# An attention block on one core: in every fourth step the weighting moves behind the scores, and all of v between the first and the second products

## The chip, the core and the metric

One core of a Trainium2 chip runs the whole program. Its engines work side by side, each on its own list of instructions, and wait for each other by semaphores: PE (TensorE, matrix products), DVE (VectorE), ACT (ScalarE), POOL (GpSimd), and SP (SyncE), which here only issues DMAs. The metric is the device time of one execution in microseconds (us). The kernel before took 781.42 us, the median of three runs (779.24 to 783.10).

## The reference

A modulated layer norm goes into attention with 16 heads over quantised weights, and a second one into a dense layer with routed low-rank experts. Shapes: x is (4, 512, 256), a head is 128 wide, features are 16 x 128.

```python
mod = (silu(c) @ wmod).reshape(4, 6, 1, 256)      # sa, ca, ga, sb, cb, gb
ga = sign(ga) * max(abs(ga), 0.25)                # gb likewise
h = layernorm(x) * (1 + ca) + sa
q, k, v = (h @ (codes_m * repeat(scales_m, 32, axis=0)) + b_m for m in "qkv")
scores = einsum("bqhd,bkhd->bhqk", q, k) / sqrt(128)
attn = softmax(scores)
out = einsum("bhqk,bkhd->bqhd", attn, v).reshape(4, 512, 2048)
x = x + ga * (out @ (wo_codes * repeat(wo_scales, 32, axis=0)) + bo)
h = layernorm(x) * (1 + cb) + sb
# 8 experts, the two best per token, weights normalised and times 16
y = h @ W.T + sum_e(weight_e(h) * (h @ A_e.T) @ B_e.T)
x = x + gb * y
```

Results are float32. The kernel keeps that precision on PE by splitting each operand into a high part (rounded) and a low part (what is left): each product is three matmuls, high x high, high x low and low x high.

## The kernel before, in words

**Steps.** Heads are taken in 8 pairs. For each pair there are 8 steps, one for each of 4 batches and 2 heads, so 64 steps in all. Step s of pair p has number n = 8p + s, and t = s % 4 is its place in a cycle of four. "First step" means t = 0 and "fourth step" t = 3. The first pair and the last are written out, the others run in a loop (pair 1 is written out on POOL, ACT and DVE too).

**What a step holds.** PE makes the scores of step n (4 tiles of 128 rows, 12 matmuls of 512 columns, function scores), the weighting of step n-2 with v (weighted, 12 matmuls of 512), v for the next step (next_v, 12 matmuls of 256) and the output projection of step n-2 (out_projection, 12 of 256). Between these lie the q and k projections of coming steps. They are made for two batches together by seven block products instead of eight, each with 3 matmuls of 512 columns for q and 3 for k (product). A fourth step has products 1 and 2 (function first_outputs), a first step products 6, 7 and 4, second and third steps one each.

**The way of a softmax tile.** DVE takes the row maximum (maximum, L1353), ACT the exponentials (exps, L887), DVE transposes blocks of 32 (turn, L1368), SP moves the blocks to their partitions with 16 DMAs a step (L449, pB to pT), ACT makes the high part (prob_high, L818), POOL the low part (prob_low, L581, tile pT_parts), and only then can PE weight (weighted waits for p_lo_ok of each of its 4 key tiles kt). The last turn of a step waits for o_mm, the end of PE's weighting in the same step.

**A fourth step before** (first_outputs, L1886): scores; product 1 for q and k, into the banks score0 and score1, each behind a wait for the exponentials of that tile (exp_ok); the weighting; product 2 for q and k, behind ACT's copies of product 1 (kept_ok); v; the output projection. The next step's scores wait for q_ok and k_ok. These come from ACT's q_high and k_high (L796, L800, after product 2) and DVE's q_low and k_low (L1250, L1255). ACT's order after the exponentials is: two copies of product 1, o_high, q_high, k_high, v_out, four high parts (first_cycle_step, prob_and_v). DVE's is: the turns, o_low, q_low, k_low, v_low, y_add (which adds the output projection to y_acc), then the next maxima.

**The last pair** has the second half's preparations on POOL and DVE. gate(b) multiplies y_acc by ga, add_gated_bo(b) adds ga * bo to x_nat, attended(b) (L1342) adds the two, statistics(b) takes row statistics and variances, inverse_std (POOL) makes 1/std, and times_gb(b) scales the dense and expert weights by gb. In step 4 of this pair DVE does attended(0) and statistics(0) between o_low and q_low. In step 7 POOL does add_gated_bo(3) and times_gb(1) to (3). After step 7 come the last two weightings (weighted_end) with low parts from DVE (hT_lo, L1348 and L1556), and then the dense layer, router and experts.

## Time and profile before

| what | value |
|---|---|
| median of 3 runs | 781.42 us (779.24 to 783.10) |
| profiled execution: its own time, its span | 782.79 us, 780.8 us |
| PE busy | 757.5 us (97%) |
| DVE, POOL, ACT busy | 660.9 (85%), 623.9 (80%), 562.5 us (72%) |
| mean granted TensorE clock | 0.995 |

The span goes from the first to the last instruction; 2.0 us of the execution's own time lie outside it. Matmuls overlap, so a busy share of PE says that it was fed and not that it ran at its peak. What shows a loss on PE is the distance between the starts of two matmuls: 0.23 us for 512 columns and 0.12 us for 256 where nothing is waited for. The granted clock is the share of full speed that PE was given.

### The profile page before, as it was taken

How to read it: one execution, taken by the hardware profiler on the slowest of the kernel's cores; microseconds unless marked ns; L12 is line 12 of the kernel's file. 1: busy time of each engine (PE TensorE's matmuls, PEld its weight loads, DVE VectorE, ACT ScalarE, POOL GpSimd, SP SyncE). 2: the span in 40 equal slices, each digit the busy share in tenths (PEclk: the TensorE clock that was granted, in tenths of full speed). 3: DMA queues.
4: the chain of work that ended last, by engine and by line, in shares of the span. 5: the costliest groups of instructions: out<-in, count | busy, mean ns of one | idle time of the engine just before them, and what ended most of it. 6: DMA issues, size and time to landing. Idle time of an engine off the chain costs nothing.

```text
span 780.8 us, 15093 instructions
## 1 busy us (share of the span) xinstructions
PE 757.5 (97%) x4128; PEld 650.9 (83%) x4128; DVE 660.9 (85%) x1268; ACT 562.5 (72%) x1226; POOL 623.9 (80%) x654
## 2 busy tenths in 40 slices
PE   8999999999999999999999999999999999989898
PEld 7888878787888888888888888888888888878697
DVE  7899989888797988888797988888797988898976
ACT  4787777777777777777777777777777777767641
POOL 4488789898688987898688987898688987988932
PEclk9999999999999999999999999999999999999999
DMA  8354434543455344543445344543445345662202
GB/s 259 91 148 125 97 81 135 136 108 94 108 142 146 91 103 128 144 125 91 112 135 151 91 104 127 141 128 91 112 135 152 91 102 133 162 176 70 49 1 108
DMA packets 71725, 92.20 MB, mean 118 GB/s; under 512 B 19477, under 2 KB 36598, under 8 KB 71670
## 3 DMA queue, kind: packets, MB, share of 16 engines
q1 hardware_dynamic: 52368, 73.21, 36.4%
q10 hardware_dynamic: 19302, 18.42, 8.0%
q8 instruction: 15, 0.25, 0.1%
q14 instruction: 40, 0.33, 0.1%
HBM read 23.39 MB, written 2.11 MB: 33 GB/s over the span
## 4 chain that ended last, share of the span: by engine, by line
PE 56%; SPq 12%; DVE 11%; issue 7%; POOL 7%; ACT 3%; DMA 2%; ACTq 1%; DVEq 0%; POOLq 0%
SPq L449 12%; PE score L1587 8%; PE score L1589 7%; PE score L1588 7%; PE o L1587 5%; PE o L1589 5%; PE o L1588 5%; POOL pT_parts L581 3%; DVE pB L1368 3%; DMA pT<-pB 2%; DVE y_acc L1322 2%; PE qv L1587 2%; PE qv L1589 2%; PE qv L1588 2%; DVE neg_max L1353 2%
## 5 line engine op out<-in xcount | busy, mean ns | idle before, releaser
L581 POOL TENSOR_TENSOR pT_parts<-pT,pT_hi 128x512 fp32r<-128x512 f32 x248 | 315.4, 1307 | 94.0 <-ACT pT_hi L818 93.9
L887 ACT ACTIVATE prob<-score,neg_max 128x512 f32<-128x512 f32 x256 | 173.3, 687 | 47.2 <-DVE neg_max L1353 45.4
L1368 DVE STREAM_TRANSPOSE pB<-prob 128x512 f32<-128x512 f32 x252 | 162.4, 686 | 48.7 <-PE o L1589 47.6
L1353 DVE TENSOR_REDUCE neg_max<-score 128x1 f32<-128x512 f32 x256 | 159.6, 680 | 1.0 <-PE score L1589 0.8
L818 ACT ACTIVATE pT_hi<-pT 128x512 fp32r<-128x512 f32 x248 | 135.6, 621 | 9.9 <-DMA pT<-pB 9.7
L1587 PE MATMUL score<-k_hi,q_hi 128*128 128x512 f32 x256 | 101.8, 398 | 3.7 <-DVE k_lo L1255 2.7
L1588 PE MATMUL score<-k_lo,q_hi 128*128 128x512 f32 x256 | 100.8, 394 | 0.0
L1589 PE MATMUL score<-k_hi,q_lo 128*128 128x512 f32 x256 | 100.3, 392 | 0.0
L1587 PE MATMUL o<-pT_hi,v_hi 128*128 128x512 f32 x248 | 96.8, 390 | 0.0
L1589 PE MATMUL o<-pT_hi,v_lo 128*128 128x512 f32 x248 | 96.6, 389 | 0.0
L1588 PE MATMUL o<-pT_parts,v_hi 128*128 128x512 f32 x248 | 96.6, 389 | 0.0
L808 ACT ACTIVATE o_hi<-o 128x512 fp32r<-128x512 f32 x62 | 37.2, 600 | 61.2 <-PE o L1589 60.9
L1587 PE MATMUL score<-wv_hi,hT_hi 128*128 128x256 f32 x228 | 64.6, 284 | 0.8 <-POOL wv_lo L656 0.8
L1589 PE MATMUL score<-wv_hi,hT_lo 128*128 128x256 f32 x228 | 64.5, 283 | 0.0
L1588 PE MATMUL score<-wv_lo,hT_hi 128*128 128x256 f32 x228 | 64.5, 283 | 0.0
L1286 DVE TENSOR_TENSOR v_lo<-score,v_hi 128x512 fp32r<-128x512 f32 x57 | 39.3, 689 | 25.2 <-ACT v_hi L804 25.2
L1587 PEld LDWEIGHTS score<-k_hi,q_hi 128*128 128x128 f32 x256 | 48.5, 189 | 13.9 <-issue 4.7
L804 ACT ACTIVATE v_hi<-score 128x512 fp32r<-128x512 f32 x57 | 34.1, 599 | 35.4 <-PE score L1589 35.1
L1589 PEld LDWEIGHTS score<-k_hi,q_lo 128*128 128x128 f32 x256 | 48.4, 189 | 10.7
L1587 PEld LDWEIGHTS o<-pT_hi,v_hi 128*128 128x128 f32 x248 | 46.5, 188 | 10.5 <-POOL pT_parts L581 0.7
L1588 PEld LDWEIGHTS score<-k_lo,q_hi 128*128 128x128 f32 x256 | 48.6, 190 | 7.5
L1589 PEld LDWEIGHTS o<-pT_hi,v_lo 128*128 128x128 f32 x248 | 46.6, 188 | 9.7
(458 smaller groups left out, 2016.1 us busy)
## 6 DMA issues: line engine op xcount, KB each, us to landing
pT<-pB SPq DMA_DIRECT2D x1008, 64.0 KB, 2.0
x_nat<-in_L_attn_x_dram ACTq DMA_DIRECT2D x4, 512.0 KB, 5.0
out_dram<-x_nat SPq DMA_DIRECT2D x8, 256.0 KB, 2.3
stage<-in_L_attn_wv_codes_dram ACTq DMA_DIRECT2D x7, 256.0 KB
stage<-in_L_attn_wv_scales_dram ACTq DMA_DIRECT2D x14, 128.0 KB
stage<-in_L_attn_wq_codes_dram ACTq DMA_DIRECT2D x7, 256.0 KB
stage<-in_L_attn_wq_scales_dram ACTq DMA_DIRECT2D x14, 128.0 KB
stage<-in_L_attn_wk_codes_dram ACTq DMA_DIRECT2D x7, 256.0 KB
```

The costliest lines, as they stand in the source:

```text
L449: sp.dma_start(flat(pT32[32 * g:32 * (g + 1), par, a]), flat(pB[32 * a:32 * (a + 1), par, g])).then_inc(p_land[par], 16)
L581: pool.tensor_tensor(turned(par, kt, pT_lo), turned(par, kt), split(pT_hi, kt).bitcast(f32), ALU.subtract).then_inc(p_lo_ok, 1)
L804: act.activation(v_hi[:, par, 2 * half:2 * half + 2, :], v_view(bank), ACT.Copy).then_inc(v_hi_ok, 1)
L808: act.activation(by_tile(o_hi[:, :]), in_token_order(bank[:, :]), ACT.Copy).then_inc(o_hi_ok, 1)
L818: act.activation(split(to, kt), turned(par, kt), ACT.Copy).then_inc(p_hi_ok, 1)
L887: act.activation(prob[:, i], score_ps[i][:, :], ACT.Exp, bias=neg_max[:, i:i + 1], accum_out=row_sum[:, s % 2, i:i + 1]).then_inc(exp_ok, 1)
L1286: dve.tensor_tensor(v_lo[:, par, tiles], v_view(bank), v_hi[:, par, tiles].bitcast(f32), ALU.subtract).then_inc(v_lo_ok, 1)
L1353: dve.tensor_reduce(neg_max[:, i:i + 1], score_ps[i][:, :], AX.X, ALU.max, negate=True).then_inc(max_ok, 1)
L1368: dve.transpose(pB[:, s % 2, :, :, i].rearrange("p g k q -> p k g q"), prob[:, i].rearrange("p (k g q) -> p k g q", k=QT, g=G)).then_inc(p ...
L1587: pe.matmul(dst, a_hi, b_hi, start=first, stop=False, skip_group_check=joins)
L1588: pe.matmul(dst, a_hi, b_lo, start=False, stop=False, skip_group_check=joins)
L1589: return pe.matmul(dst, a_lo, b_hi, start=False, stop=last, skip_group_check=joins)
```

## The change

1. Fourth steps, PE (first_outputs): the weighting comes straight behind the scores, then product 1, then both tiles of v, then product 2, then the output projection.
2. Fourth steps, ACT: o_high before the copies of product 1, v_out before q_high and k_high; the high part of the v weights (v_weights_high, steps 7) behind the exponentials instead of before them. DVE: v_low before q_low and k_low.
3. POOL, steps 1 and 2 of each pair from pair 1 on: the low parts of the mixed q and k (mixed_low, L570) before the parts of the output weights instead of behind them.
4. First pair: in step 6 POOL's first q part waits for q_mm alone, and ACT makes the high part of input mix 4 behind the four high parts of the weights; in step 7 DVE's input_mix(0, 3) goes from before the last turn to behind o_low.
5. Last pair: POOL's add_gated_bo(2) in step 4 waits for attended(0) (x1_ok); DVE's variances(0) go behind k_low; in step 7 POOL does times_gb(1) and then waits for DVE's four low parts (p_lo_dve); add_gated_bo(3), times_gb(2) and times_gb(3) go further back.

The same computation is done; no instruction is added or taken away on PE, DVE, ACT or POOL but for waits.

```diff
@@ POOL, first pair
                     elif s == 6:
                         input_mix_lo(0, 2)
+                        pool.wait_ge(q_mm, SPP)
+                        parts_1("q", 1)
                         pool.wait_ge(k_mm, SPP)
-                        parts_1("q", 1)
                         parts_1("k", 1)
@@ POOL, pair
                     elif s < 3:
+                        for m in "qk":
+                            mixed_low(m, u3 if s == 1 else u2, mixed)
                         pool.wait_ge(y_mm, DC * (n - 2))
                         parts("o", p, 2 - s)
...
                         elif s == 4:
                             gate(0)
+                            pool.wait_ge(x1_ok, 1)
                             add_gated_bo(2)
...
                         else:
-                            add_gated_bo(3)
                             times_gb(1)
-                            times_gb(2)
-                            times_gb(3)
+                            pool.wait_ge(p_lo_dve, QT)
...
-                    if s % 4 in (1, 2):
+                    if s in (5, 6):
                         for m in "qk":
-                            mixed_low(m, u3 if s % 4 == 1 else u2, mixed)
+                            mixed_low(m, u3 if s == 5 else u2, mixed)
@@ POOL, after the last pair
             inverse_std(B + 1)
+            add_gated_bo(3)
             gate(2)
...
             pool.tensor_tensor(x_nat[:, rows], y_acc[:, rows], x_nat[:, rows], ALU.add).then_inc(x1_ok, 1)
+            times_gb(2)
             inverse_std(B + 2)
+            times_gb(3)
             inverse_std(B + 3)
@@ ACT, first_cycle_step
                 made = cycle(p, s // 4) + 1
+                o_high(n - 1)
                 first_copied("q", made + 1)
                 first_copied("k", made + 1)
-                o_high(n - 1)
+                v_out(n + 2, batch_of((s + 1) % SPP) % 2, (s + 1) % 2)
                 q_high(SPP + 2 * made + 1, 0, first_ps["q"])
                 k_high(SPP + 2 * made + 1, 0, first_ps["k"])
                 if isinstance(p, int) and p == 0:
                     input_mix_hi(0, 3)
-                prob_and_v(p, s)
+                prob_high((s - 1) % 2, landed(p, s - 1))
@@ DVE, pair
                     if last and s == 4:
                         attended(0)
-                        statistics(0)
+                        for i in range(QT):
+                            row_statistics(0, i)
...
                         k_low(SPP + 2 * now, head_at(p, s + 1))
+                        if last and s == 4:
+                            variances(0)
                     elif t == 3:
+                        v_low(n + 2, batch_of(nxt) % 2, nxt % 2)
                         q_low(SPP + 2 * now + 1, head_at(p, s + 1), first_ps["q"])
                         k_low(SPP + 2 * now + 1, head_at(p, s + 1), first_ps["k"])
-                    v_low(n + 2, batch_of(nxt) % 2, nxt % 2)
+                    if t < 3:
+                        v_low(n + 2, batch_of(nxt) % 2, nxt % 2)
@@ PE, first_outputs
+                weighted_ready(p, s)
+                weighted(n - 2, s % 2, batch_of(s - 2) % 2, j)
                 for i, m in enumerate("qk"):
                     if s == SPP - 1:
                         pe.wait_ge(w_ok[m], parts_of(m, p + 1) + 1)
                     pe.wait_ge(exp_ok, QT * n + i + 1)
                     product(first_ps[m], m, 1, b, True).then_inc(product_mm[m], 1)
-                weighted_ready(p, s)
-                weighted(n - 2, s % 2, batch_of(s - 2) % 2, j)
+                next_v(p, s)
                 for m, done in (("q", q_mm), ("k", k_mm)):
                     pe.wait_ge(kept_ok[m], kept("copy", made))
                     product(first_ps[m], m, 2, b, False).then_inc(done, 1)
-                next_v(p, s)
                 out_projection(p, s)
```

PE at the end of the scores in the fourth step of the loop's first half (score<-k is a score matmul, score<-hT_hi,wq_hi a matmul of product 1, o<-pT_hi one of the weighting). Before:

```order
L1589 MATMUL score<-k_hi,q_lo 128x512
L1892 ISA
L1893 REGISTER_ALU
L1587 MATMUL score<-hT_hi,wq_hi 128x512
L1588 MATMUL score<-hT_lo,wq_hi 128x512
L1589 MATMUL score<-hT_hi,wq_lo 128x512
```

And of the changed kernel, at the same place and then from the end of v:

```order
L1597 MATMUL score<-k_hi,q_hi 128x512
L1598 MATMUL score<-k_lo,q_hi 128x512
L1599 MATMUL score<-k_hi,q_lo 128x512
L1597 MATMUL o<-pT_hi,v_hi 128x512
L1598 MATMUL o<-pT_parts,v_hi 128x512
L1599 MATMUL o<-pT_hi,v_lo 128x512
```

```order
L1599 MATMUL score<-wv_hi,hT_lo 128x256
L1909 ISA
L1597 MATMUL score<-hT_hi,wq_hi 128x512
L1598 MATMUL score<-hT_lo,wq_hi 128x512
L1599 MATMUL score<-hT_hi,wq_lo 128x512
L1597 MATMUL score<-hT_hi,wk_hi 128x512
L1598 MATMUL score<-hT_lo,wk_hi 128x512
L1599 MATMUL score<-hT_hi,wk_lo 128x512
L1867 MATMUL y<-wo_hi,o_hi 128x256
L1868 MATMUL y<-wo_lo,o_hi 128x256
```

The weighting, which stood six matmuls behind the last score matmul, is now its neighbour, and product 2 has only the output projection between it and the next scores.

ACT in the fourth step of the last pair (o_hi is o_high, qv and ky from score the copies of product 1). Before:

```order
L887 ACTIVATE prob,row_sum<-score,neg_max 128x512 x4
L823 ACTIVATE qv<-score 128x512
L823 ACTIVATE ky<-score 128x512
L808 ACTIVATE o_hi<-o 128x512
L796 ACTIVATE q_hi<-score,bias_now 128x512
L800 ACTIVATE k_hi<-score,bias_now 128x512
L804 ACTIVATE v_hi<-score 128x512
L818 ACTIVATE pT_hi<-pT 128x512 x4
```

And of the changed kernel:

```order
L892 ACTIVATE prob,row_sum<-score,neg_max 128x512 x4
L813 ACTIVATE o_hi<-o 128x512
L828 ACTIVATE qv<-score 128x512
L828 ACTIVATE ky<-score 128x512
L809 ACTIVATE v_hi<-score 128x512
L801 ACTIVATE q_hi<-score,bias_now 128x512
L805 ACTIVATE k_hi<-score,bias_now 128x512
L823 ACTIVATE pT_hi<-pT 128x512 x4
```

o_hi moved before the two copies, and v_hi before q_hi and k_hi.

DVE in step 4 of the last pair (x_nat<-y_acc,x_nat is attended(0), BN_STATS to var_eps the statistics). Before:

```order
L1291 TENSOR_TENSOR o_lo<-o,o_hi 128x512
L1342 TENSOR_TENSOR x_nat<-y_acc,x_nat 128x1024
L1148 BN_STATS stats<-x_nat 128x6 x4
L1154 BN_AGGR mv<-stats 128x2 x4
L1159 TENSOR_SCALAR var_eps<-mv 128x4
L1250 SCALAR_TENSOR_TENSOR q_lo<-qv,vecT,q_hi 128x512
L1255 SCALAR_TENSOR_TENSOR k_lo<-ky,vecT,k_hi 128x512
L1286 TENSOR_TENSOR v_lo<-score,v_hi 128x512
```

And of the changed kernel:

```order
L1297 TENSOR_TENSOR o_lo<-o,o_hi 128x512
L1348 TENSOR_TENSOR x_nat<-y_acc,x_nat 128x1024
L1154 BN_STATS stats<-x_nat 128x6 x4
L1256 SCALAR_TENSOR_TENSOR q_lo<-qv,vecT,q_hi 128x512
L1261 SCALAR_TENSOR_TENSOR k_lo<-ky,vecT,k_hi 128x512
L1160 BN_AGGR mv<-stats 128x2 x4
L1165 TENSOR_SCALAR var_eps<-mv 128x4
L1292 TENSOR_TENSOR v_lo<-score,v_hi 128x512
```

The variances moved from before q_lo to behind k_lo; attended(0) and the row statistics stay where they were.

## Rows read from the trace of the kernel before

**Rows 1.** The page, busy time, share of the span and instructions of each engine:

```profile
PE 757.5 (97%) x4128; PEld 650.9 (83%) x4128; DVE 660.9 (85%) x1268; ACT 562.5 (72%) x1226; POOL 623.9 (80%) x654
```

**Rows 2.** Who waited for whom on PE: us in total, times, longest:

```profile
PE score L1587 <- ACT prob L887: 10.3, 14, 1.5
...
PE score L1587 <- DVE k_lo L1255: 2.7, 1, 2.7
```

**Rows 3.** PE in order of time, one fourth step: start us, us, engine, line, operation:

```profile
408.07 0.40 PE L1587 MATMUL score<-k_hi,q_hi 128*128 128x512 f32 x1
...
410.60 0.39 PE L1589 MATMUL score<-k_hi,q_lo 128*128 128x512 f32 x1
...
411.64 0.50 PE L1587 MATMUL score<-hT_hi,wq_hi 128*128 128x512 f32 x1 [0.66 <-ACT prob L887]
...
411.98 0.39 PE L1588 MATMUL score<-hT_lo,wq_hi 128*128 128x512 f32 x1
...
417.00 0.39 PE L1589 MATMUL score<-hT_hi,wk_lo 128*128 128x512 f32 x1
...
420.10 0.40 PE L1587 MATMUL score<-k_hi,q_hi 128*128 128x512 f32 x1
```

**Rows 4.** In order of time, the weights' low parts against the scores, two fourth steps:

```profile
408.83 5.06 POOL L581 TENSOR_TENSOR pT_parts<-pT,pT_hi 128x512 fp32r<-128x512 f32 x4 [1.52 <-ACT pT_hi L818]
...
451.95 0.40 PE L1587 MATMUL score<-k_hi,q_hi 128*128 128x512 f32 x1
...
452.63 5.05 POOL L581 TENSOR_TENSOR pT_parts<-pT,pT_hi 128x512 fp32r<-128x512 f32 x4 [1.45 <-ACT pT_hi L818]
```

**Rows 5.** The chain that ended last, in order of time: start us, us, what:

```profile
439.76 0.72 DVE pB L1368
...
449.91 1.98 DMA pT<-pB
```

**Rows 6.** In order of time, the end of k in a first step:

```profile
430.16 0.39 PE L1589 MATMUL ky<-gb_row_parts,wk_lo 128*128 128x512 f32 x1
...
431.32 0.75 DVE L1255 SCALAR_TENSOR_TENSOR k_lo<-ky,vecT,k_hi 128x512 fp32r<-128x512 f32 x1
```

**Rows 7.** In order of time, v in the fourth step of the first pair:

```profile
104.48 1.28 POOL L656 TENSOR_TENSOR wv_lo<-stage,wv_hi 128x512 fp32r<-128x512 f32 x1
...
105.81 0.39 PE L1587 MATMUL score<-wv_hi,hT_hi 128*128 128x256 f32 x1 [0.77 <-POOL wv_lo L656]
```

**Rows 8.** In order of time, the last pair's fifth step into its sixth:

```profile
692.31 2.40 POOL L607 TENSOR_TENSOR x_nat<-x_nat,ga_bo 128x1024 f32<-128x1024 f32 x1
...
692.44 3.35 DVE L1342 TENSOR_TENSOR x_nat<-y_acc,x_nat 128x1024 f32<-128x1024 f32 x1
...
697.68 1.19 DVE L1159 TENSOR_SCALAR var_eps<-mv 128x4 f32<-128x4 f32 x1
...
699.45 0.73 DVE L1255 SCALAR_TENSOR_TENSOR k_lo<-ky,vecT,k_hi 128x512 fp32r<-128x512 f32 x1
...
700.44 0.47 PE L1587 MATMUL score<-k_hi,q_hi 128*128 128x512 f32 x1 [2.67 <-DVE k_lo L1255]
```

**Rows 9.** Stretches: busy time and instructions by engine, PEclk, DMA share, GB/s:

```profile
188.00:192.00 4.00, 2.63 (x12) 1.86 (x11) 3.79 (x9) 3.80 (x9) 3.13 (x3) 1.00 0.44 107
...
702.00:705.30 3.30, 3.30 (x9) 2.57 (x8) 2.71 (x5) 2.12 (x6) 1.89 (x4) 0.52 0.45 111
```

**Rows 10.** In order of time, the last weightings of the tail:

```profile
733.11 5.22 DVE L1348 TENSOR_TENSOR hT_lo<-pT,hT_hi 128x512 fp32r<-128x512 f32 x4 [1.17 <-ACT hT_hi L818]
...
733.16 1.78 POOL L614 TENSOR_TENSOR u<-stage,gb_row 128x512 f32<-128x512 f32 x1
...
733.86 0.50 PE L1587 MATMUL ky<-hT_hi,v_hi 128*128 128x512 f32 x1 [0.65 <-DVE hT_lo L1348]
...
743.01 0.40 PE L1589 MATMUL o<-hT_hi,v_lo 128*128 128x512 f32 x1
...
751.35 1.23 DVE L1342 TENSOR_TENSOR x_nat<-y_acc,x_nat 128x1024 f32<-128x1024 f32 x1
```

More of the change, by code:

```diff
@@ L943, in first_pair @@
                             act.dma_start(gate_dram[:, i], gate_rows_out[i]).then_inc(gate_kept, 16)
-                    if s == SPP - 1:
-                        v_weights_high(0)
                     if start:
@@ L953, in first_pair @@
                     if s == SPP - 1:
+                        v_weights_high(0)
                         first_cycle_step(0, s)
@@ L988, in first_pair @@
                         act.activation(modT[:, GB:GB + DC], mod_columns(GB - GA, DC), ACT.Copy).then_inc(mod_ok, 1)
-                    if s in (5, 6):
-                        input_mix_hi(0, (2, 4)[s - 5])
+                    if s == 5:
+                        input_mix_hi(0, 2)
                     if s == SPP - 2:
@@ L995, in first_pair @@
                     if s == SPP - 2:
+                        input_mix_hi(0, 4)
                         next_bias(0)
@@ L1009, in pair @@
                         ffn_normalise(0)
-                    if s == SPP - 1 and not last:
-                        v_weights_high(p)
                     if end:
@@ L1036, in pair @@
                         exps(n, s, range(QT))
+                        if s == SPP - 1:
+                            v_weights_high(p)
                         first_cycle_step(p, s)
@@ L1405, in first_pair @@
                     turn(0, s, 2)
-                    if s == SPP - 1:
-                        input_mix(0, 3)
                     turn(0, s, 3)
@@ L1411, in first_pair @@
                         o_low(n - 1)
+                    if s == SPP - 1:
+                        input_mix(0, 3)
                     if s == 2:
@@ L1416, in first_pair @@
                     if s == SPP - 1:
+                        v_low(SPP + 1, 0, 0)
                         q_low(SPP + 1, head_at(0, SPP), first_ps["q"])
@@ L1432, in first_pair @@
                         v_low(SPP, batch_of(SPP - 1) % 2, (SPP - 1) % 2)
-                    elif s == SPP - 1:
-                        v_low(SPP + 1, 0, 0)
                     if not early:
```

## The prediction

> **What bounds the kernel now.** I read the busy shares first. PE is busy for 97% of the span [rows 1], and its clock is granted nearly throughout, so PE sets the time and only its gaps can be won. The list of PE's waits comes next [rows 2]: 14 waits of 10.3 us in all for the exponentials, and one of 2.7 us for k_lo. Then I read a fourth step in order of time [rows 3]. Its scores start at 408.07 and the twelfth score matmul at 410.60, 0.23 us apart. Product 1 could follow at 410.83 and starts at 411.64, 0.81 us late. The first matmul after a gap also holds up the next: they stand 0.34 us apart and not 0.23. So such a step loses 0.92 us. This happens in the 14 fourth steps that have product 1: one in the first pair, one in the last, two in each of the six between.
>
> The weighting can fill that gap only if its operands are there. POOL makes the four low parts from 408.83 on, in 5.06 us, so the fourth is ready at 413.89 [rows 4]. Before, the weighting stood behind the six matmuls of product 1, so by the same pace it started at 413.1 and came to its fourth tile at 415.2, where nothing was waited for. What sets the time of those low parts is the chain that ended last [rows 5]. DVE's last transpose of the second step before ends at 440.48, and the blocks land at 451.89, 11.4 us later, in which SP issues its 16 DMAs and the last of them lands. ACT's high part and POOL's low part follow. The place where this chain starts (DVE's work in the first and second steps of the cycle) is not touched by the change.
>
> **Part 1: weighting behind the scores, fourth steps.** PE comes to the fourth weighting tile nine matmuls behind 410.83, at 412.88. It is ready at 413.89. With 0.1 us for PE to react and 0.11 us for the slow restart this is a loss of 1.22 us; the shorter wait for the third tile is inside it. In the step that starts at 451.95, the same working gives 456.76 wanted, 457.68 ready [rows 4], and a loss of 1.13 us. Mean 1.17 us, where 0.92 to 1.00 us (mean 0.96) was lost for the exponentials. Those are ready long before product 1 now. So the wait is exchanged and not removed: +0.21 us a step. The bounds: 0 for the new wait if the low parts came in time, and 1.5 us if every one of the two tiles pays its own restart and reaction.
>
> **Part 2: v before product 2.** Before, the last matmul of product 2 started at 417.00 and the next scores at 420.10 [rows 3]; the 3.1 us between were v (12 x 0.12 = 1.43) and the output projection (1.44). ACT and DVE turned product 2 into q_lo and k_lo beneath them. Now only the output projection is left as cover: the scores could start 0.23 + 1.44 = 1.67 us after that matmul. A first step shows how long k takes from its last matmul when ACT and DVE are free. The matmul starts at 430.16 and k_lo ends at 432.07 [rows 6], 1.91 us. PE then needed 0.26 us from the end of k_lo (700.18) to its scores at 700.44 [rows 8]. So the scores come 2.17 us after, 0.50 us late, and 0.08 us more for the slow restart: 0.58 us a step, in 13 steps (the first pair is counted below). v_out stands in front of q_high on ACT now, but v ends 1.4 us before product 2 does, and ACT's copy is through by then. Behind k_lo on DVE stands y_add and then the maxima of the next scores. They start with the scores as before, so they hand on nothing more. Bounds: 0 if the chain is 0.5 us shorter, 0.9 us if v_out collides.
>
> **The sum over the fourth steps.** The ten steps of pairs 2 to 6 look like the two shown: 0.21 + 0.58 = 0.79 us each, 7.9 us. The three others (two in pair 1, one in the last pair) had other gaps, in pair 1 one of 1.37 us within four [rows 9], and the low parts come later where the exponentials did. The exchange in part 1 then comes out between -0.5 and +0.2 us; I take 0.5 us each in all, between 0.1 and 0.8: 1.5 us. In the first pair v waited for its low weights, until 105.81 [rows 7]. POOL ends them at 105.76. PE now comes to v earlier, stands there for some 2 us until about 105.4 or 105.8, and has product 2 (1.36 us) still before it, with 0.58 us before the scores: +1.5 us. Together +10.9 us.
>
> **Part 3: the last pair's fifth step.** DVE's attended(0) took 3.35 us beside POOL's add of 2.40 us [rows 8], and the same operation 1.23 us with POOL idle [rows 10]. It and the statistics delayed k_lo to 700.18, and PE stood 2.67 us. Some time after, PE's clock fell to 0.52 of full, near its lower level of 1.2 GHz, for 3.3 us, in which 9 matmuls started instead of 14 [rows 9]: 1.2 us. Now POOL waits for attended(0), which saves DVE 2.1 us, and the variances, whose last instruction alone took 1.19 us, go behind k_lo. k_lo ends at about 696.5, before PE wants it at 697.6. The gap, its restart and the slow clock go: -4.1 us. POOL's add moves back by 1.4 us and ends near 697, about when ACT's high parts are there for POOL's next work, so I count nothing for it. What is late next is y_add before the fourth score tile, at 699.4 against 699.7, so just in time; at worst it returns 0.9 us.
>
> **Part 4: the tail.** DVE's four last low parts took 5.22 us beside POOL's 1.78 us operations [rows 10]; by the same two durations of attended they take about 0.65 each alone. PE needed from 733.86 to 743.01 for 24 matmuls that take 5.2 us at their pace, 3.9 us of waits. Half of these stay, for DVE's y_add lies between: -2.5 us. But POOL now does add_gated_bo(3), whose larger half takes 2.4 us as in rows 8, before the sum for batch 2, and times_gb(3) stands beside DVE's gate and sum for batch 3, so the last batch's normalised rows are late: +0.6 us, at worst +2.5. Part 3 and 4 make -6.0 us (-3.5 to -7).
>
> The Trainium skill, "SBUF — State Buffer", section "Who interferes with whom", says that a VectorE instruction with two SBUF inputs contends with a GpSimd one that reads SBUF, and one with a single SBUF input does not. By that, q_lo and k_lo (one input is PSUM) would be free beside POOL's add, but gate(3) and attended(3) would each pay for times_gb(3), up to 2 us of part 4. The trace agrees with the first half by the 3.35 against 1.23 us; no row here shows the second.
>
> **The other changes.** The mixed low parts earlier, the first pair's input mixes and v_weights_high lie beside ACT's high parts, which POOL waited for (1.5 us idle before its low parts [rows 4]), so I count 0; with that cover gone, the parts of the output weights (1.4 us) would push prob_low.
>
> **Sum.** 10.9 - 6.0 = +4.9 us on the execution's own 782.79 us: 787.7. That execution is 1.4 us above the median of 781.42, so on the median's scale I predict **786.3 us**. What a measurement of this kernel can tell from no change is about 0.5%, 3.9 us; so "slower" begins at 785.3 and "faster" below 777.5.
>
> **The rivals.**
> - *A, the gap is filled:* the low parts are in time, because the cycle shifts under them. Then the 14 us lost in the fourth steps go (10.3 us of waits [rows 2] and some 0.25 us each for reaction and restart), and 0.58 us a step comes, 7.5 us: 781.4 - 6.5 - 6.0 = 768.9. For it: the first tile is ready at 410.14, before 410.83. Against it: the fourth is not, by 1.0 us in every step [rows 4]. 8%.
> - *B, no wait for k_lo:* ACT and DVE get 0.5 us faster through it. 10.9 - 13 x 0.58 = 3.4, less 6.0: 778.8. Against it is the 1.91 us of rows 6. 17%.
> - *C, the last pair gives nothing:* y_add or the late batch returns what parts 3 and 4 save. 792.3. The margins of 0.3 us speak for it. 12%.
> - *D, the clock:* two waits within ten microseconds let the clock fall in each fourth step as it fell behind the 2.67 us gap. At 1.2 us each, 13 times, this is 16 us more: 802. Against it: in a stretch of pair 1 PE stood for 1.37 of 4 us and its clock stayed at 1.00 [rows 9], and gaps of 0.8 us left it alone in every fourth step. 3%. The Trainium skill, "TensorE: Matmul & The Clock Gate", section "A second HAM failure mode: psum-queue depth-cycling", says that frequent short idling between groups of matmuls can make the clock go up and down; that would be D, and the trace has not shown it for gaps of this size.
>
> **How the numbers follow.** The forecast has 60%, with its own range from 783 to 790. A part of it lies under 785.3, a third. Slower: 40 of the forecast, 12 of C and 3 of D, 55%. Same: 19 of the forecast and 13 of B, 32%. Faster: 8 of A, 4 of B and 1 of the forecast, 13%. The range that should hold 8 in 10 leaves out A (8), D (3), half of C (6) and the lower edge of B (3): 778 to 792.
>
> **What would show it.** In the profile after, PE should wait inside the weighting of the fourth steps, released by POOL's pT_parts, 0.9 to 1.1 us in 13 steps, and at the next scores for DVE's k_lo, about 0.4 to 0.5 us. The waits for prob should be gone, and attended(0) near 1.23 us with no 2.7 us gap and no clock dip behind it. I am wrong if pT_parts doesn't appear among PE's waits (A), if k_lo doesn't (B), or if the last 90 us are not some 6 us shorter (C).

## The result and the profile after

The changed kernel takes 789.94 us, the median of four runs (788.91 to 790.91), against 782.01 us for the kernel before (779.24 to 783.10). The ratio is 1.0104 with an interval from 1.0079 to 1.0128: some 6 to 10 us slower. The profiled execution has a span of 787.9 us.

The page, busy time by engine (answers to [rows 1]):

```profile
PE 760.3 (96%) x4128; PEld 651.5 (83%) x4128; DVE 658.9 (84%) x1268; ACT 564.6 (72%) x1226; POOL 622.7 (79%) x654
```

Who PE waited for, in total, times, longest (answers to [rows 2]):

```profile
PE y L1867 <- POOL wo_lo L512: 8.7, 7, 1.7
PE o L1597 <- POOL pT_parts L581: 3.5, 13, 0.3
PE score L1597 <- DVE k_lo L1261: 2.6, 6, 0.5
PE score L1597 <- POOL wv_lo L657: 2.1, 1, 2.1
```

The 14 waits for the exponentials (10.3 us) are gone, and so is the one of 2.7 us. Two of the new names I had forecast (pT_parts, k_lo), and one I had forecast for the first pair (wv_lo). The largest, wo_lo, I had not: it is the low part of the output weights, and it is waited for once a pair. The 13 waits for pT_parts are not one in each of 13 steps, as I had forecast: there are two in the eighth step of each of pairs 1 to 6 and one in the last pair's fourth step, and none in the fourth steps of pairs 1 to 6.

The distances between the starts of steps on PE show where the time went. They are worked out from the first score matmul of each step in the two profiles; for pairs 2 to 6, which agree within 0.3 us, the mean of five:

| stretch | before | after | difference |
|---|---|---|---|
| first pair, eighth step | 12.67 | 15.89 | +3.22 |
| pair 1, all eight steps | 91.50 | 91.32 | -0.18 |
| pairs 2 to 6, third step (s = 2) | 9.70 | 11.18 | +1.48 |
| fourth step (s = 3) | 12.01 | 11.42 | -0.59 |
| eighth step (s = 7) | 12.13 | 12.83 | +0.70 |
| first and fifth step | 12.44 | 12.53 | +0.09 each |
| last pair, s = 4 and 5 | 27.74 | 23.32 | -4.42 |
| from step 63's start to the end | 58.49 | 56.89 | -1.60 |

A pair of the loop gets 1.76 us longer. The third step, which holds no reordered PE instruction, pays most of it. In order of time there (start us, us, engine, line, operation, in brackets the idle time before and who ended it):

```profile
411.18 1.30 POOL L570 TENSOR_TENSOR k_lo<-u,k_hi 128x512 fp32r<-128x512 f32 x1
...
413.13 0.72 POOL L512 TENSOR_TENSOR wo_lo<-stage,wo_hi 128x256 fp32r<-128x256 f32 x1
413.91 0.38 PE L1867 MATMUL y<-wo_hi,o_hi 128*128 128x256 f32 x1 [1.23 <-POOL wo_lo L512]
...
415.44 0.40 PE L1597 MATMUL score<-k_hi,q_hi 128*128 128x512 f32 x1
```

POOL now makes the mixed low parts first and the parts of the output weights behind them, so wo_lo ends at 413.85, and out_projection of s == 2 stands 1.23 us: it is the one place where PE waits for these parts. Two lines of out_projection:

```python
                if s == 2:
                    pe.wait_ge(w_ok["o"], 2 * p + 2)
```

The fourth step starts at 415.44. Its weighting finds every low part ready, since PE came 1.5 us later: it takes 11.42 us, less than before. The wait that I had priced at 1.17 us a step is paid there one step earlier and under another name.

The eighth step, in order of time (answers to [rows 3] and [rows 4]):

```profile
459.46 5.04 POOL L581 TENSOR_TENSOR pT_parts<-pT,pT_hi 128x512 fp32r<-128x512 f32 x4 [1.46 <-ACT pT_hi L823]
...
463.31 0.50 PE L1597 MATMUL o<-pT_hi,v_hi 128*128 128x512 f32 x1 [0.26 <-POOL pT_parts L581]
...
464.56 0.50 PE L1597 MATMUL o<-pT_hi,v_hi 128*128 128x512 f32 x1 [0.29 <-POOL pT_parts L581]
...
469.33 0.39 PE L1599 MATMUL score<-hT_hi,wk_lo 128*128 128x512 f32 x1
...
470.60 0.75 DVE L1261 SCALAR_TENSOR_TENSOR k_lo<-score,vecT,k_hi 128x512 fp32r<-128x512 f32 x1
...
471.61 0.49 PE L1597 MATMUL score<-k_hi,q_hi 128*128 128x512 f32 x1 [0.47 <-DVE k_lo L1261]
```

Here the forecast holds. Step 39 starts at 458.79, so at the scores' pace the fourth tile would be due twenty-one matmuls later, at 463.6; it starts at 464.56. The profile's brackets show only 0.26 and 0.29 us of that, since matmuls overlap; the distance between starts shows all of it. From the last matmul of product 2 to the next scores it is 2.28 us, and the wait for k_lo is the last 0.47.

The first pair's eighth step (answers to [rows 7]):

```profile
102.93 1.71 POOL L657 TENSOR_TENSOR wv_lo<-stage,wv_hi 128x512 fp32r<-128x512 f32 x1
...
104.70 0.38 PE L1597 MATMUL score<-wv_hi,hT_hi 128*128 128x256 f32 x1 [2.10 <-POOL wv_lo L657]
...
111.08 0.49 PE L1597 MATMUL score<-k_hi,q_hi 128*128 128x512 f32 x1 [0.34 <-DVE k_lo L1261]
```

And its stretches: busy time and instructions of PE, PEld, DVE, ACT, POOL, then the granted clock, the DMA share and GB/s:

```profile
104.70:106.00 1.30, 1.30 (x7) 1.30 (x8) 0.00 (x0) 0.00 (x0) 1.18 (x1) 0.64 0.49 114
106.00:108.00 2.00, 2.00 (x10) 1.81 (x8) 0.00 (x0) 0.60 (x1) 0.00 (x0) 0.50 0.17 40
108.00:109.50 1.50, 1.50 (x9) 1.27 (x7) 0.82 (x2) 0.84 (x2) 0.00 (x0) 0.84 0.36 87
```

The wait for wv_lo was forecast, the fall of the clock to its lower level behind it (0.50 of 2.4 GHz) was not.

The last pair's fifth step and the tail (answers to [rows 8] and [rows 10]):

```profile
705.02 1.21 DVE L1348 TENSOR_TENSOR x_nat<-y_acc,x_nat 128x1024 f32<-128x1024 f32 x1
...
708.24 0.75 DVE L1261 SCALAR_TENSOR_TENSOR k_lo<-ky,vecT,k_hi 128x512 fp32r<-128x512 f32 x1
...
710.19 0.40 PE L1597 MATMUL score<-k_hi,q_hi 128*128 128x512 f32 x1
...
741.61 2.49 DVE L1354 TENSOR_TENSOR hT_lo<-pT,hT_hi 128x512 fp32r<-128x512 f32 x4
```

attended(0) takes 1.21 us, k_lo ends at 708.99, over a microsecond before PE starts its scores, and the gap is gone. DVE's four low parts of the tail take 2.49 us instead of 5.22, and PE's last weighting starts its last matmul 17.77 us behind step 63's start instead of 20.70. From there to the end it is 39.12 us instead of 37.79: part of the gain is paid back. There DVE's gate(3) and attended(3) stand beside POOL's times_gb(3) and take 2.17 and 1.64 us instead of 1.23 each, and PE waits 1.71 us for the normalised rows of the last batch:

```profile
757.32 2.17 DVE L1340 TENSOR_TENSOR y_acc<-y_acc,stage 128x1024 f32<-128x1024 f32 x1
759.52 1.64 DVE L1348 TENSOR_TENSOR x_nat<-y_acc,x_nat 128x1024 f32<-128x1024 f32 x1
...
766.13 0.65 PE L1797 MATMUL qv<-ident,z 128*128 128x128 f32 x4 [1.71 <-DVE z L1182]
```

### The profile page after: what moved, and what is told of

It reads as the page before. It is cut to its first block, busy times and chain, and to the rows that moved or that the text cites. A ratio compares the mean times of both kernels' runs of the same rounds, so it can differ in the third digit from the quotient of the medians.

```text
span 787.9 us, 15087 instructions
## 1 busy us (share of the span) xinstructions
PE 760.3 (96%) x4128; PEld 651.5 (83%) x4128; DVE 658.9 (84%) x1268; ACT 564.6 (72%) x1226; POOL 622.7 (79%) x654
## 4 chain that ended last, share of the span: by engine, by line
POOL 31%; PE 30%; issue 14%; DVE 11%; SPq 7%; ACT 4%; DMA 2%; ACTq 1%; POOLq 0%; DVEq 0%
POOL pT_parts L581 15%; SPq L449 7%; PE score L1597 4%; PE score L1599 4%; PE score L1598 4%; POOL stage L499 2%; POOL k_lo L570 2%; PE o L1597 2%; POOL q_lo L570 2%; PE o L1598 2%; PE o L1599 2%; DVE pB L1374 2%; DVE neg_max L1359 2%; DMA pT<-pB 2%; PE qv L1597 1%
## 5 line engine op out<-in xcount | busy, mean ns | idle before, releaser
L1597 PE MATMUL o<-pT_hi,v_hi 128*128 128x512 f32 x248 | 98.5, 397 | 3.7 <-POOL pT_parts L581 3.5
L1328 DVE SCALAR_TENSOR_TENSOR y_acc<-y,inv_sum,y_acc 128x256 f32<-128x256 f32 x118 | 51.2, 476 | 6.9 <-PE y L1872 5.6
```

The lines of the kernel that those rows point to most:

```text
L1328: dve.scalar_tensor_tensor(out=rows, in0=y_view(t, banks), scalar=inv_sum[:, ring, t:t + 1], in1=rows, op0=ALU.mult, op1=ALU.add).then_inc ...
L1597: pe.matmul(dst, a_hi, b_hi, start=first, stop=False, skip_group_check=joins)
```

## The experiments

Twelve runs in four groups (e1, e2, e4, e5; e3, e6, e7, e8; e9 to e11; e12); kernels of one group ran on one chip beside the kernel before, whose median was 781.15, 781.32 and 780.80 us in the first three. Medians:

| kernel | us | ratio to before, 95% |
|---|---|---|
| e1: output weights first again | 788.16 | 1.0095 (1.0074 to 1.0116) |
| e2: second tile of v behind product 2 | 784.14 | 1.0040 (1.0024 to 1.0055) |
| e5: before, with mixed low parts first | 786.03 | 1.0062 (1.0040 to 1.0083) |
| e4: before, with the weighting in two halves | 766.94 | 0.9814 (0.9791 to 0.9838) |
| e3: before, with the last pair's edits | 775.68 | 0.9932 (0.9905 to 0.9959) |
| e6: e3 and e4 together | 765.43 | 0.9798 (0.9771 to 0.9824) |
| e7: low part of wv early | 786.90 | 1.0067 (1.0041 to 1.0094) |
| e8: e6 with the low part of wv early | 764.49 | 0.9783 (0.9758 to 0.9808) |
| e9: before, POOL's add waits | 779.88 | 0.9991 (0.9972 to 1.0009) |
| e10: before, variances behind k_low | 781.10 | 1.0005 (0.9980 to 1.0029) |
| e11: changed kernel with e1, e2 and e7 | 778.21 | 0.9971 (0.9956 to 0.9986) |
| e12: e10 again, one run | 781.09 | none |

### e1: is the wait for wo_lo a loss of its own?

```diff
                     elif s < 3:
-                        for m in "qk":
-                            mixed_low(m, u3 if s == 1 else u2, mixed)
                         pool.wait_ge(y_mm, DC * (n - 2))
                         parts("o", p, 2 - s)
...
-                    if s in (5, 6):
+                    if s % 4 in (1, 2):
```

> The changed kernel with one edit undone: in steps 1 and 2 of each pair POOL makes the parts of the output weights first again, and the low parts of the mixed q and k behind them. My theory T: in the changed kernel PE waits 1.2 to 1.7 us in each third step for the low part of the output weights, and comes 1.5 us later to the fourth step of the first half, so that the low parts of the weighting are there without a wait. With the edit undone the third step goes from 11.18 back to 9.70 us, and the fourth step from 11.42 to about 12.8 us, because the wait for pT_parts that I had predicted comes back there. Net -0.1 us a pair: 789 us, within 0.3% of the changed kernel. Rival R (the wait for the output weights costs its whole length, nothing is given back): -1.5 us in each of 6 pairs, -0.3 more in pair 1: 780.5 us, about the time of the kernel before.

788.16 us, 1.8 less than the changed kernel by the medians and 0.7 by the ratios, where the rival asked for nine. The third step of pairs 2 to 6 is back at 9.70 us, and the fourth takes 12.60 to 12.80 us. PE's weighting in that fourth step:

```profile
417.78 0.50 PE L1595 MATMUL o<-pT_hi,v_hi 128*128 128x512 f32 x1 [0.28 <-POOL pT_parts L581]
...
419.02 0.51 PE L1595 MATMUL o<-pT_hi,v_hi 128*128 128x512 f32 x1 [0.28 <-POOL pT_parts L581]
```

These are the two waits of the eighth step, now in the fourth too; the list has 24 of them, 6.6 us, instead of 13. So in the changed kernel one wait stands for the other, and the edit costs hardly anything there. This fourth step is also the one that the prediction described: 12.01 + 0.79 = 12.80 us forecast, 12.68 on the mean of pairs 2 to 6.

### e5: the same edit alone, on the kernel before

```diff
                     elif s < 3:
+                        for m in "qk":
+                            mixed_low(m, u3 if s == 1 else u2, mixed)
                         pool.wait_ge(y_mm, DC * (n - 2))
                         parts("o", p, 2 - s)
...
-                    if s % 4 in (1, 2):
+                    if s in (5, 6):
                         for m in "qk":
-                            mixed_low(m, u3 if s % 4 == 1 else u2, mixed)
+                            mixed_low(m, u3 if s == 5 else u2, mixed)
```

> The kernel before with one edit alone: in steps 1 and 2 of each pair POOL makes the low parts of the mixed q and k before the parts of the output weights. PE's order is that of before. My theory T: PE's output projection in the third step waits for the low part of the output weights as in the changed kernel, +1.2 to 1.5 us in each of 7 pairs, and here nothing gives it back, for the weighting stands behind product 1 and waits for nothing: +9 to +10 us, 791.5 us. Rival R (the count of my prediction: these edits lie beside ACT's high parts and cost nothing): 782 us.

786.03 us: neither. The edit does cost something, but half of what I expected. The third step takes 11.20 us (+1.50), with the same gap:

```profile
406.88 0.39 PE L1859 MATMUL y<-wo_hi,o_hi 128*128 128x256 f32 x1 [1.25 <-POOL wo_lo L512]
```

The fourth step, though, takes 11.07 to 11.14 us instead of 12.01: its wait for the exponentials is gone. ACT in order of time, before and then here:

```profile
410.82 0.67 ACT L887 ACTIVATE prob<-score,neg_max 128x512 f32<-128x512 f32 x1
```

```profile
410.19 0.69 ACT L889 ACTIVATE prob<-score,neg_max 128x512 f32<-128x512 f32 x1 [0.47 <-DVE neg_max L1355]
```

Before, this first exponential came 2.75 us behind the step's first score matmul (408.07), because ACT was still at its high parts and a copy behind them until 410.8; here it comes 1.78 us behind (408.41), and what it waits for is only DVE's maximum. PE's hold of 1.25 us lets ACT catch up, which gives 0.93 us back. Net 0.57 us a pair, 2.9 us in pairs 2 to 6, and 1.3 us in the last pair, where less came back: 4.2 us; measured 4.9 (3.1 to 6.5). Pair 1 is left out of this sum. It is 1.5 us shorter than before in this profile (90.00 against 91.50), but its steps differ by more than that between executions of one kernel (see e9 and e12 below).

### e2: the cover for q_lo and k_lo

```diff
-                next_v(p, s)
+                next_v_tile(p, s, 0)
                 for m, done in (("q", q_mm), ("k", k_mm)):
                     pe.wait_ge(kept_ok[m], kept("copy", made))
                     product(first_ps[m], m, 2, b, False).then_inc(done, 1)
+                next_v_tile(p, s, 1).then_inc(v_mm, 1)
                 out_projection(p, s)
```

ACT's v_out goes behind k_high and DVE's v_low behind k_low with it.

> The changed kernel with the second tile of v behind product 2 in every fourth step (on PE; v_out behind k_high on ACT and v_low behind k_low on DVE again). The first tile stays between the products. My theory T: it gives q_lo and k_lo 0.72 us more cover, so the wait for k_lo at the next scores goes: -0.5 us in each eighth step, -0.2 us in each fourth step of the first half, and -0.5 us in the first pair, about -5 us in all: 785 us. Rival R (product 2 then waits for ACT's copies of product 1, 0.3 to 0.5 us, or v_out and v_low come too late for the scores of the next step): what is gained is lost again, 789 to 791 us.

784.14 us: 5.8 less than the changed kernel by the medians, 5.0 by the ratios. No wait for k_lo is left in the list of PE's waits:

```profile
PE y L1866 <- POOL wo_lo L512: 8.7, 7, 1.7
PE o L1596 <- POOL pT_parts L581: 3.4, 13, 0.3
PE score L1596 <- POOL wv_lo L657: 2.1, 1, 2.1
```

The eighth step goes from 12.83 to 12.20 us, the fourth from 11.42 to 11.08, and the steps behind them from 12.53 to 12.45. So part 2 is worth 0.63 us in an eighth step (forecast 0.58), and what remains there, 12.20 against 12.13 before, is part 1: the exchange of one wait for the other costs 0.07 us (forecast 0.21). Before the scores behind a fourth step the changed kernel's profile shows 0.18 us of idle time and names no releaser; in e2 that too is gone.

### e7: the gap in the first pair and the clock

```diff
+                        v_weights_low(0)
                         parts_s23("q", 1)
                         parts_s23("k", 1)
-                        v_weights_low(0)
                         input_mix_lo(0, 4)
```

> The changed kernel with one edit: in the last step of the first pair POOL makes the low part of the v weights before the parts of the sums for q and k instead of behind them. ACT's high part is ready at 100.8 us, so POOL ends it near 102.2 instead of 104.6 us. My theory T: PE's wait of 2.10 us at v goes, and with it the stretch at half clock that follows it (0.50 in 106 to 108 us): the step goes from 15.89 to about 12.9 us, 787 us in all. Rival R1 (the clock falls for another cause, such as the weight loads there): only the 2.1 us of the wait go, the granted clock still falls, 788 us and a step of 13.8 us. Rival R2 (the parts of the sums, now 1.3 us later, are late for product 6 of the next step): the wait moves there, 789 to 790 us.

786.90 us: 3.0 less by the medians, 2.9 by the ratios. In order of time, POOL and the next scores:

```profile
101.19 1.30 POOL L657 TENSOR_TENSOR wv_lo<-stage,wv_hi 128x512 fp32r<-128x512 f32 x1 [0.70 <-ACT wv_hi L911]
...
107.47 0.49 PE L1597 MATMUL score<-k_hi,q_hi 128*128 128x512 f32 x1 [0.34 <-DVE k_lo L1261]
```

The stretches behind v, columns as above:

```profile
104.00:106.00 2.00, 2.00 (x13) 1.74 (x12) 0.92 (x2) 1.55 (x3) 1.92 (x4) 1.00 0.43 102
106.00:108.00 2.00, 1.66 (x12) 1.41 (x11) 2.00 (x5) 2.00 (x5) 1.31 (x2) 1.00 0.23 53
```

The step takes 12.00 us instead of 15.89, where I had expected 12.9; nothing waits for the parts that moved back, and the clock stays at 1.00. Of the 3.9 us the gap and its restart are 2.2; the other 1.7 were matmuls at the lower clock. 0.3 us came back in pair 1, and the step before ended 0.3 us later.

### e11: the three together

> The changed kernel with all three costs mended: the parts of the output weights first in steps 1 and 2, the second tile of v behind product 2, the low part of the v weights early in the first pair. What is left of the change beside before is the weighting behind the scores and the edits of the last pair and the tail. My theory T: no wait for wo_lo, k_lo or wv_lo; the third step is 9.70 us; the fourth of the first half keeps the wait for the low parts in full, 12.65 less 0.35 for k_lo, 12.3 us against 12.03 before; the eighth is 12.2 against 12.13. So this is the kernel before with the last pair's edits (775.7 us) plus 0.35 us in each of 6 or 7 pairs: 778 us. Rival R (the single gains add up from 789.9 us: 1.8, 5.8 and 3.0 us): 779.3 us; and if the waits for the low parts grow where the other waits are gone, 782 us.

778.21 us, against 789.94 for the changed kernel. From 200 to 620 us PE waits for one thing only:

```profile
PE o L1594 <- POOL pT_parts L581: 5.0, 18, 0.3
```

On the mean of pairs 2 to 6 the fourth step takes 12.27 us and the eighth 12.22, as my theory said. The weighting behind the scores thus costs 0.26 + 0.09 us a pair more than the order before, though k has the cover that e2 gave it back: some 2 us in all. Beside the 775.68 of e3 it is 2.5, but that comparison is not clean: e11 also has the low part of wv early, which e3 has not (the first pair's eighth step takes 11.49 us against 12.69), and its pair 1 is 2.2 us longer in the profiles. The time alone can't tell my theory from the rival's 779.3, since by its ratio e11 lies at 779.2; the steps do. The wait for the exponentials has only been replaced.

### e4: half of the weighting in the gap

In this cut weighted takes its key tiles as the last argument.

```diff
+                weighted_ready(p, s)
+                weighted(n - 2, s % 2, batch_of(s - 2) % 2, j, range(2))
                 for i, m in enumerate("qk"):
...
                     product(first_ps[m], m, 1, b, True).then_inc(product_mm[m], 1)
-                weighted_ready(p, s)
-                weighted(n - 2, s % 2, batch_of(s - 2) % 2, j)
+                weighted(n - 2, s % 2, batch_of(s - 2) % 2, j, range(2, QT))
```

> The kernel before with one edit: in every fourth step the first two key tiles of the weighting stand behind the scores, then product 1, then the other two tiles, then product 2, v and the output projection as before. My theory T: the gap of 0.92 to 1.00 us before product 1 (the wait for the exponentials and the slow restart) is filled, since the first tile's low part is ready at 410.14 and the second's at about 411.4 where PE wants them at 410.83 and 411.5, and the third and fourth (412.7 and 413.9) are wanted at 413.6 and 414.3. v still covers q_lo and k_lo. So -0.9 us in 13 or 14 fourth steps: -12 us, 770 us. Rival R (the wait moves on: everything shifts 0.9 us earlier on PE while POOL's and SP's chain for the low parts does not, so the same 0.9 us is waited for at the fourth tile or in the next step): 780 to 782 us.

766.94 us, 14.2 less than before. PE and POOL in the fourth step that starts at 404.21:

```profile
404.99 5.07 POOL L581 TENSOR_TENSOR pT_parts<-pT,pT_hi 128x512 fp32r<-128x512 f32 x4 [1.55 <-ACT pT_hi L818]
...
406.73 0.39 PE L1589 MATMUL score<-k_hi,q_lo 128*128 128x512 f32 x1
406.96 0.39 PE L1587 MATMUL o<-pT_hi,v_hi 128*128 128x512 f32 x1
...
408.39 0.40 PE L1587 MATMUL score<-hT_hi,wq_hi 128*128 128x512 f32 x1
...
409.77 0.39 PE L1587 MATMUL o<-pT_hi,v_hi 128*128 128x512 f32 x1
```

No bracket is left: from 200 to 620 us the profile shows no wait of PE at all. A fourth step takes 11.08 to 11.15 us, and its 36 matmuls of 512 columns and 24 of 256 need 36 x 0.23 + 24 x 0.12 = 11.2 us at their pace. The first two tiles are what is ready when the scores end, and product 1 gives POOL the time for the other two. A pair of the loop is 1.92 us shorter than before (85.98 against 87.90), which is 9.6 us in pairs 2 to 6. Most of the rest does not come from the gap before product 1: the last pair is 4.4 us shorter, since the gap of 2.67 us and the slow clock behind it are gone there too (below).

### e3, e6, e8: the last pair's edits, and the sum

> The kernel before with the edits of the last pair and the tail alone (POOL's add waits for attended(0), the variances behind k_low, add_gated_bo(3), times_gb(2) and times_gb(3) further back). My theory T (parts 3 and 4 of the prediction): the fifth step of the last pair goes from 16.36 to about 13.6 us and the next from 11.38 to 9.7 us, because the gap of 2.67 us and the slow clock behind it go; the tail gains 1.6 us; step 6 gets 0.6 us longer. -5.4 us: 776 us. Rival R (in the changed kernel the gap went because its fourth steps shift PE against POOL, not by these edits): the gap stays, 779 to 781 us. For the rival speaks that the kernel with the weighting in two halves and none of these edits had no such gap either: its fifth step took 13.54 us.

> The weighting in two halves around product 1 (as in the earlier experiment, 766.94 us) with the edits of the last pair and the tail. My theory T: the last pair's fifth step is already at 13.5 us in that kernel, so only the tail's gain is left, -1.6 us, and step 6 gets nothing: 765.3 us. Rival R (the full gain of 5.4 us adds up): 761.5 us.

> The weighting in two halves around product 1, the edits of the last pair and the tail, and the low part of the v weights early in the last step of the first pair. My theory T: beside the kernel without the last of these it loses the wait of 1.34 us for that low part: 764 us. Rival R: no difference from it, since v there has cover elsewhere: 765.3 us.

e3 is the kernel before with item 5 of the change alone, e6 adds that to e4, and e8 is e6 with the POOL edit of e7. e3 takes 775.68 us; its fifth and sixth steps in the last pair take 13.53 and 9.70 us, the seventh 11.16, and 56.9 us follow step 63's start: the figures of the changed kernel to 0.1 us. So these edits make that gain by themselves, 5.6 us (3.2 to 7.4). e6 takes 765.43 us and e8 764.49. Their ratios overlap with each other's and e4's, so only the traces tell them apart: the first pair's eighth step takes 12.65 us in e6 and 11.06 in e8, which has no wait for wv_lo. e8 beats both kernels, by 2.2% (1.9 to 2.4) the one before.

In e4 the gap in the last pair is gone without any edit there. In order of time:

```profile
682.25 1.34 DVE L1342 TENSOR_TENSOR x_nat<-y_acc,x_nat 128x1024 f32<-128x1024 f32 x1
...
682.59 3.25 POOL L607 TENSOR_TENSOR x_nat<-x_nat,ga_bo 128x1024 f32<-128x1024 f32 x1
```

DVE's attended(0) started first here and took 1.34 us, and POOL's add 3.25. In [rows 8] POOL had started 0.13 us before DVE and took 2.40, and DVE 3.35. Each pays for coming second, POOL 0.85 us and DVE 2.1.

### e9, e10, e12: which of the last pair's edits does it?

e9 has POOL's wait for x1_ok alone, e10 the variances behind k_low alone, e12 is e10 again.

```diff
                             gate(0)
+                            pool.wait_ge(x1_ok, 1)
                             add_gated_bo(2)
```

> The kernel before with one edit: in the fifth step of the last pair POOL's add of ga times bo waits until DVE's attended(0) is done. The variances stay before q_low. My theory T: attended(0) takes 1.2 to 1.3 us instead of 3.35, so k_lo ends 2.1 us earlier (698.1), PE's scores start 2.1 us earlier and the gap is 0.5 us instead of 2.67; behind it the clock stays up. The step goes from 16.36 to 14.2 us and the next from 11.38 to 9.8 us: 777.5 us. Rival R1 (the add, now later, slows the variances that follow, 1.19 us for a tiny instruction, even more): only 1.0 to 1.5 us are won, 779.5 us. Rival R2 (the clock falls whatever the gap is): step of 14.2, next of 11.4, 779.2 us.

> The kernel before with one edit: in the fifth step of the last pair DVE's variances(0) go behind k_low. POOL's add doesn't wait. My theory T: attended(0) still takes 3.35 us beside the add; k_lo ends 1.6 us earlier (0.38 + 1.19 us of variances), so the gap is 1.1 us instead of 2.67, and a gap of that size left the clock up in each third step of the changed kernel: the step goes to 14.8 us, the next to 9.8 us: 778 us. Rival R (the clock falls behind this gap too, as behind the one of 2.67 us): step of 14.8, next of 11.4 us, 779.7 us.

> The same kernel as in the run with the variances alone moved behind k_low, for a second profile: its median of 781.1 us doesn't fit its first profile, which was of a short execution (777.36 us) and shows the last pair's fifth and sixth steps 2.8 us shorter than before. Theory T: executions of this kernel (775.2 to 784.4 us) differ in the steps of pair 1 and in the last 100 us, where DVE and POOL start operations on shared ground within some 0.1 us of each other; an execution near or above the median shows one of these places 2 to 4 us longer, and the fourth steps of pairs 2 to 6 unchanged at 12.0 to 12.1 us. Rival R: all steps are longer by some 0.1 us each in the long executions, a matter of the loop and not of single places.

Both medians miss my theory: 779.88 and 781.10 us, no difference from before. e9's lies near rival R1's 779.5, but its fifth step won 1.9 us and not the 1.0 to 1.5 of that rival. The traces agree with the steps all the same. In e9 the last pair's fifth and sixth steps take 14.46 and 9.76 us, in e10 14.65 and 10.29, against 16.36 and 11.38, and behind e10's gap of 0.96 us the granted clock is 1.00 from 696 to 704 us, which speaks against its rival. DVE in e9, then in e10 and e12:

```profile
694.25 1.21 DVE L1343 TENSOR_TENSOR x_nat<-y_acc,x_nat 128x1024 f32<-128x1024 f32 x1
...
697.35 1.42 DVE L1160 TENSOR_SCALAR var_eps<-mv 128x4 f32<-128x4 f32 x1
```

```profile
695.42 0.17 DVE L1159 TENSOR_SCALAR var_eps<-mv 128x4 f32<-128x4 f32 x1
```

```profile
698.07 1.31 DVE L1159 TENSOR_SCALAR var_eps<-mv 128x4 f32<-128x4 f32 x1
```

e12, an execution of 781.09 us, has fourth steps of 12.0 to 12.1 us in pairs 2 to 6 like e10's first profile (777.36 us). It is longer in single places: by 1.17 us in the fourth step of pair 1 (13.23 against 12.06), 0.78 us in its eighth, and 1.10 us in the last pair's sixth (11.39 against 10.29), where PE waits 0.49 us for v_lo and 0.63 for y_acc, the DVE work behind the var_eps that took 1.31 us instead of 0.17. So executions of one kernel differ there, as my theory said. In e9's profile the fourth step of pair 1 takes 14.90 us, behind this gap:

```profile
146.30 0.50 PE L1588 MATMUL score<-hT_hi,wq_hi 128*128 128x512 f32 x1 [1.92 <-ACT prob L888]
```

From step 63 on, e9, e10 and e12 also take 0.5 to 0.6 us more than before (59.0 and 59.1 against 58.5). PE stands there once for 1.8 us, where the longest such wait before was 0.73; in e10:

```profile
728.95 0.50 PE L1590 MATMUL ky<-hT_hi,v_hi 128*128 128x512 f32 x1 [1.81 <-DVE hT_lo L1348]
```

Behind it the granted clock is 0.52 from 730 to 733 us, 0.51 from 734.4 to 737 us in e9, and 0.60 from 732.7 to 737 us in e12. Neither this nor one or two profiles of each settles why two edits that save 3.5 and 2.8 us in their traces leave the medians where they were. What the last pair's edits bring is shown for all of them together (e3), not divided.

## Why the prediction was right, and where it was wrong

The time came out at 789.94 us, 3.6 us above the 786.3 forecast and inside its range; "slower" was the likeliest of the three. The difference came out at +7.9 us by the medians where +4.9 was forecast: 0.6 us of the 3.6 lie in the median of the kernel before, 782.01 here and 781.42 there.

- **Part 1, the exchange of waits.** The mechanism holds in the eighth steps: the low parts end 5.71 us behind the step's first scores, 5.73 before [rows 4], and the wait for the exponentials goes. The exchange costs +0.07 us by e2 and +0.09 by e11, where +0.21 was forecast. In the fourth step of the first half it doesn't show in the changed kernel, because PE has been held one step earlier; with that taken away it is there (e1: 12.68 us, e11: 12.27). The sign that I had named, a wait in each of 13 steps, was thus seen in seven.
- **Part 2, v before product 2.** Right in mechanism, and in size in the eighth steps: 0.63 us by e2 for 0.58 forecast. In the fourth steps it is 0.34, where I had counted 0.58 as well.
- **The step that failed is "the other changes ... I count 0".** I had named the mixed low parts among them and had said what they would push: "the parts of the output weights (1.4 us) would push prob_low". I looked for the next thing on POOL's own list, and not for who waits for the parts: PE's output projection of s == 2, with its wait for w_ok["o"]. It costs 1.48 us in each third step. The cover that I had named, ACT's high parts, stands behind these parts on POOL and covers nothing that PE wants before.
- **The sum over the loop came near by a second error.** That wait gave back 0.6 us in each next step. I had 10 x 0.79 = 7.9 us for pairs 2 to 6; measured are 5 x 1.76 = 8.8, and so close only by luck. For the three other fourth steps I had 1.5 us; pair 1 is 0.2 us shorter and the first four steps of the last pair 1.6 us longer. With the first pair's 3.1 us this makes 13.3 us for the 10.9 forecast. (The start of the last pair moved by 10.9 us, but that figure leaves out the last pair's 1.6 and holds 0.85 us by which the first scores start earlier in the profile after, 17.00 against 17.85; over all profiles this start lies between 17.0 and 18.4. Its agreement is luck too.) That the two errors offset each other is shown by e1, which removes the wait and leaves the time within 0.3%.
- **The first pair.** +1.5 us forecast for its eighth step, +3.2 found. The mis-sized term is the stretch at the lower clock behind a gap of 2.10 us, which I had seen behind the one of 2.67 us in part 3 and did not carry over (e7).
- **Parts 3 and 4.** -4.1 forecast and -4.4 found for the fifth and sixth steps; 0.6 us comes back in the seventh. (The pair's third and fourth steps are 1.1 and 0.4 us longer; the third is wo_lo again.) The tail is 1.6 us shorter (forecast 1.9): 2.9 won up to the last weighting where 2.5 was forecast, and 1.3 paid behind it where 0.6 was. That payment is the late last batch that I had named; gate(3) and attended(3), for which the prediction had no row, took 2.17 and 1.64 us beside times_gb(3) against 1.23 each. e3 gives -5.6 us for -6.0.
- **The rivals.** A did not come: the low parts stayed late, and where they were in time, in the fourth steps of the first half, PE had waited one step earlier; B did not, as k_lo is waited for; C did not, as the last stretch is shorter. D did not, as the waits inside the fourth and eighth steps left the clock alone. The clock fell in the first pair, but behind the one wait for wv_lo, which D did not name.

## What to carry to other kernels

When an instruction moves back on an engine, look up the consumers of everything that is pushed behind it, not only what is next on that engine: every semaphore it raises, and where each is first waited for. A wait removed or added on the critical engine changes the next one, because the others catch up meanwhile; price edits in pairs, and test one with the other taken away. And when an operand is late by a fixed time, a gap is filled best with the part of the work that is already ready: half of the weighting saved 1.92 us a pair (e4) where all of it cost 0.35 (e11).

## What the runs showed of the hardware

- The clock fell behind gaps of 1.81 us (e10's tail, granted 0.52 from 730 to 733 us), 1.92 us (e9, 0.67 from 146 to 150 us), 2.10 us (changed kernel, 0.50) and 2.67 us (before, [rows 9]). It stayed at 1.00 behind gaps of 1.23 us (changed kernel, 413 to 417 us), 1.34 us (e4, first pair, 104 to 108 us), 1.71 us (changed kernel's tail, 766 to 770 us) and 1.73 us (changed kernel, pair 1, 143 to 148 us). What the fall costs is what is left of e7's 3.9 us when the gap of 2.10 us and its restart are taken off: some 1.7 us.
- Two large additions on DVE and POOL, both with two inputs in SBUF, cost the one that starts second: 3.35 us (before) against 1.21 (e9) for DVE's, 3.25 (e4) against 2.40 (before) for POOL's, and 0.13 or 0.34 us of difference in the start decided which. The Trainium skill, "SBUF — State Buffer", section "Who interferes with whom", says that issue order decides who blocks; the runs agree.
- An operation of 128x4 elements on DVE took 0.17 us in one execution (e10) and 1.31 us in another of the same kernel (e12), beside POOL's low parts both times.
